# Staging of the last batch's h1 and h2 weights in two places by turns, in a two-layer transformer kernel

## The reference, cut to what matters

```python
def _L1_ffn_ref(x, w1_w, w1_s, w2_w, w2_s, h1_w, h1_s, h2_w, h2_s, w3_w, w3_s):
    h = silu(_tlin(x, w1_w, w1_s)) * _tlin(x, w2_w, w2_s)   # 256 -> 1024
    h = gelu(_tlin(h, h1_w, h1_s), approximate=False)       # 1024 -> 1024
    h = gelu(_tlin(h, h2_w, h2_s), approximate=False)       # 1024 -> 1024
    return _tlin(h, w3_w, w3_s)                             # 1024 -> 256
```

## Time and profile before

| What | Value |
|---|---|
| Median of 3 runs | 2720.88 us |
| The runs | 2719.23, 2720.88, 2723.3 us |
| The profiled execution's own time | 2726.29 us |
| Its span | 2724.6 us |
| Mean granted clock of TensorE in it | 0.927 |
| Busy, of the span | PE 86%, DVE 64%, ACT 55%, POOL 45% |
| Instructions | 27484 |
| Share of the DMA engines, queue q1 | 46.0%, 355.80 MB |

### The profile page before, as it was taken

The page is one execution under the profiler, slowest core; times in us unless marked ns, Lnnn a source line. Parts: engine busy times, 40 slices in busy tenths (PEclk is TensorE's granted clock), DMA queues, the critical chain, the costliest instruction groups (busy, mean ns, idle before and its releaser), DMA issues.

```text
span 2724.6 us, 27484 instructions
## 1 busy us (share of the span) xinstructions
PE 2330.2 (86%) x8452; PEld 1465.7 (54%) x8452; DVE 1748.2 (64%) x2782; ACT 1505.2 (55%) x1982; POOL 1226.2 (45%) x974
## 2 busy tenths in 40 slices
PE   2898989989989846778998998988988988998977
PEld 1456656567566622234554555555555555565666
DVE  3445464555454337899679679689689689687620
ACT  0232433425324225547877876876867866877733
POOL 1232251332422214556556556565556555556622
PEclk6899999999999867888999999998999999999988
DMA  7034534454445533444655645645645544647522
GB/s 227 0 119 137 166 124 133 150 162 132 136 137 155 174 110 108 119 117 131 171 133 131 170 133 134 171 132 129 175 129 134 171 128 138 160 133 176 151 83 78
DMA packets 381907, 374.34 MB, mean 137 GB/s; under 512 B 22369, under 2 KB 308593, under 8 KB 381761
## 3 DMA queue, kind: packets, MB, share of 16 engines
q1 hardware_dynamic: 375616, 355.80, 46.0%
q0 software_dynamic: 6144, 16.79, 2.0%
HBM read 335.45 MB, written 37.06 MB: 137 GB/s over the span
## 4 chain that ended last, share of the span: by engine, by line
PE 20%; DVE 13%; issue 11%; ACT 9%; DMA 6%; POOL 4%; SPq 1%; DVEq 0%; POOLq 0%; ACTq 0%
DMA w_stage<-h_T 5%; PE bank L1441 5%; PE bank L223 4%; DVE bank L1366 4%; PE bank L229 4%; PE bank L230 4%; DVE w_st L1374 4%; POOL d_in L1356 2%; ACT w_ring L1597 2%; ACT bank L1421 2%; DVE cv L1192 2%; ACT L1421 2%; PE bank L1674 1%; POOL f1L L1543 1%; PE bank L1675 1%
## 5 line engine op out<-in xcount | busy, mean ns | idle before, releaser
L1356 POOL TENSOR_TENSOR d_in<-u,bc 128x512 f32<-128x512 f32 x512 | 665.5, 1314 | 452.2 <-DMA bc<-bc_rows 327.7
L1366 DVE TENSOR_TENSOR_SCAN bank<-bank,d_in 128x512 f32<-128x512 f32 x512 | 624.7, 1221 | 185.7 <-ACT bank L1421 156.9
L1441 PE MATMUL bank<-w_st,ident 128*128 128x512 f32 x1024 | 544.8, 646 | 120.2 <-DVE w_st L1374 120.1
L1421 ACT ACTIVATE bank<-dt,a_neg 128x512 f32<-128x512 f32 x512 | 348.4, 687 | 292.9 <-DVE w_st L1374 291.0
L229 PE MATMUL bank<-f1H,w_ring 128*128 128x512 f32 x768 | 355.2, 462 | 34.8 <-POOL f1L L1543 23.8
L1441 PEld LDWEIGHTS bank<-w_st,ident 128*128 128x128 f32 x1024 | 194.2, 201 | 353.9 <-DVE w_st L1374 226.6
L1374 DVE TENSOR_TENSOR w_st<-bank,bc 128x512 f32<-128x512 f32 x512 | 343.9, 673 | 53.0 <-PE bank L1441 52.8
L230 PE MATMUL bank<-f1L,w_ring 128*128 128x512 f32 x768 | 311.3, 405 | 0.0
L229 PE MATMUL bank<-f0H,w_ring 128*128 128x512 f32 x512 | 230.2, 450 | 11.2 <-POOL f0L L1543 5.9
L1597 ACT ACTIVATE w_ring<-w_stage 128x1024 fp32r<-128x1024 f32 (+1 forms) x192 | 173.0, 905 | 112.6 <-DMA w_stage<-h_T 50.9
L1543 POOL TENSOR_TENSOR f0L<-mid,f0H 128x512 fp32r<-128x512 f32 x128 | 170.6, 1334 | 134.6 <-ACT f0H L1626 78.7
(11 more groups left out here) (202 smaller groups left out, 3898.5 us busy)
## 6 DMA issues: line engine op xcount, KB each, us to landing
bc<-bc_rows SPq DMA_DIRECT2D x256, 512.0 KB, 5.1
w_stage<-h_T SPq DMA_DIRECT2D x256, 256.0 KB, 3.4
w_exp<-L_ffn_ew SPq DMA_DIRECT2D x240, 256.0 KB, 4.6
w_stage<-w_T SPq DMA_DIRECT2D x128, 128.0 KB, 2.8
eo_rows<-eo SPq DMA_DIRECT2D x56, 256.0 KB, 4.3
xs<-xs_rows SPq DMA_DIRECT2D x24, 512.0 KB, 4.0
xA<-L_attn_x SPq DMA_DIRECT2D x8, 512.0 KB, 6.4
x_mid<-xA SPq DMA_DIRECT2D x8, 512.0 KB, 2.9
```

The costliest lines, as they stand in the source:

```text
L1356: pool.tensor_tensor(d_in[:, nth(b, s) % IN, :], u[:, c, :], rows_tile(b, use)[:, 0, :], ALU.mult).then_inc(in_made.sem, 1)
L1366: dve.tensor_tensor_scan(bank[:, :], bank[:, :], d_in[:, nth(b, s) % IN, :], 0.0, ALU.mult, ALU.add).then_inc(scanned.sem, 1)
L1421: act.activation(state_bank(b, s)[:, :], dt[:, c, :], ACT.Exp, scale=a_neg[:, c, n:n + 1]).then_inc(dA_made.sem, 1)
L1441: pe.matmul(y_bank(c)[:, :], ident[:, :], w_st[:, nth(b, s) % WG, :], start=False, stop=(n == NST - 1)).then_inc(summed.sem, 1)
```

## The change

For the last batch (`b == B - 1`) and the hidden steps (w >= 8), even steps are staged in `w_stage` as before and odd steps in `late_stage`, the first two thirds of `d_in`. The DMAs of step w then wait for the cast of w - 2 instead of w - 1 (step 8 still waits for all casts of the first eight, step 9 for the last scan of the batch), and their due time is that of the cast of w - 2. Both DMAs of a step count on the semaphore of its place. The other seven batches are issued as before.

```diff
@@ -1465,8 +1465,16 @@
 
 
 
-            def stage_part(w):
-                return w_stage[:, 4 * (w % 2):4 * (w % 2) + 4, :] if w < KF else w_stage[:, :, :]
+
+            late_stage = d_in[:, 0:2, :].rearrange("p a s -> p (a s)").rearrange("p (k n) -> p k n", n=P)
+
+            def by_turns(b, w):
+                return b == B - 1 and w >= KF
+
+            def stage_part(b, w):
+                if w < KF:
+                    return w_stage[:, 4 * (w % 2):4 * (w % 2) + 4, :]
+                return late_stage if by_turns(b, w) and w % 2 else w_stage[:, :, :]
 
             def ring_part(w):
                 if w < KF:
@@ -1477,6 +1485,8 @@
 
                 if w < KF:
                     return [stage_in[w % 2].at(b, 32 * (w // 2 + 1))]
+                if by_turns(b, w):
+                    return [stage_in[w % 2].at(b, 32 * KF // 2 + 32 * ((w - KF) // 2 + 1))]
                 return [stage_in[j].at(b, 32 * KF // 2 + 16 * (w - KF + 1)) for j in range(2)]
 
             def ring_freed(b, w):
@@ -1497,8 +1507,12 @@
                     yield 0
                     sp.dma_start(w3_stage, k_tiles(ins["w3_T"])).then_inc(w3_in.sem, 16)
                 for w in range(3 * KF):
-                    yield cast_at(b, w - (2 if w < KF else 1)) + PLAN["stage"]
-                    if w >= KF:
+                    yield cast_at(b, w - (2 if w < KF or by_turns(b, w) else 1)) + PLAN["stage"]
+                    if w == KF + 1 and by_turns(b, w):
+                        sp.wait_ge(*scanned.all(b))
+                    elif w > KF + 1 and by_turns(b, w):
+                        sp.wait_ge(*ring_made.at(b, w - 1))
+                    elif w >= KF:
                         sp.wait_ge(*ring_made.at(b, w))
                     elif w >= 2:
                         sp.wait_ge(*ring_made.at(b, w - 1))
@@ -1507,12 +1521,13 @@
                     m = slice(w % KF * P, (w % KF + 1) * P)
                     if w < KF:
                         for j, name in enumerate(("w1_T", "w2_T")):
-                            sp.dma_start(stage_part(w)[:, KD * j:KD * (j + 1), :], k_tiles(ins[name])[:, :, m]
+                            sp.dma_start(stage_part(b, w)[:, KD * j:KD * (j + 1), :], k_tiles(ins[name])[:, :, m]
                                          ).then_inc(stage_in[w % 2].sem, 16)
                     else:
                         for j in range(2):
                             k = slice(KF // 2 * j, KF // 2 * (j + 1))
-                            sp.dma_start(w_stage[:, k, :], k_tiles(ins[f"h{w // KF}_T"])[:, k, m]).then_inc(stage_in[j].sem, 16)
+                            there = stage_in[w % 2 if by_turns(b, w) else j]
+                            sp.dma_start(stage_part(b, w)[:, k, :], k_tiles(ins[f"h{w // KF}_T"])[:, k, m]).then_inc(there.sem, 16)
 
             def out_sync(b):
                 yield mlp_at(b) + 40
@@ -1594,7 +1609,7 @@
                         act.wait_ge(*there)
                     if b or w >= 4:
                         act.wait_ge(*ring_freed(b, w))
-                    act.activation(ring_part(w), stage_part(w), ACT.Copy).then_inc(ring_made.sem, 1)
+                    act.activation(ring_part(w), stage_part(b, w), ACT.Copy).then_inc(ring_made.sem, 1)
 
             def mlp_scalar(b):
                 M = mlp_at(b)
```

## The result

The changed kernel took 2702.9 us in the median of 4 runs (2698.73 to 2704.74), the kernel before 2720.12 in the median of 4 beside it; the ratio is 0.9932, with a 95% interval of 0.9915 to 0.995. The profiled execution took 2703.35 us with a span of 2701.6.

What follows compares the result with a forecast made beforehand. One staging place with a serial round was taken to bound the last batch's hidden steps: 25.4 + 2.9 + 5.4 + 25.4 + 2.9 = 62.0 us against 76.4. Gain 14.4, less 2.1 for luck, gave 2708.6 us, range 2703 to 2714.

Steps and rivals of the forecast that it cites:

- The mechanism: Last batch's hidden steps: the staging round of 4.82 us exceeds a 3.63 us tile; DMAs one cast earlier remove the landing.
- The queue of SP: Last batch: step 8's DMAs go ahead of the gbM load, moving it from 2618.0 to about 2621.7; cost nothing.
- The sum: First hidden tile after the opening one to last product: 62.0 us against 76.4, gain 14.4, with 5.4 for h2's first tile.
- Against the median: Whole kernel: half of 4.2 us taken off as the profiled execution's luck, so gain 12.3 and 2708.6 us.
- the late landing: Round before the cast for h1's last tile: 6.08 us instead of 4.82, counted as 1.26 us of luck.
- T7's clock: Last tile of h1, partly at 1.2 GHz: 5.36 us instead of 3.63, counted as 1.73 us of luck.
- T8's longer spell: First tile of h2, longer at 1.2 GHz: 6.62 us against 5.38, counted as 1.24 us of luck.
- Short pauses cost no clock: Rival: h2's first tile takes 3.63 us instead of 5.38 after its pause, time 2706.9; chance 0.12.
- Landings that share the engines: Rival: two steps in flight double each landing, 4.0 us a tile, 5 us given back, 2713.6; chance 0.07.
- ScalarE's order: Rival: odd casts behind two tiles' Gelus come late, PE waits at 7 odd tiles, 8.4 us back, 2717.0; chance 0.06.
- a clock that falls under steady load: Rival: hidden tiles without pauses run at 1.2 GHz, 3.0 us more each; with six, 2726.6; chance 0.03.
- no effect: Rival: last batch's DMAs still go out one at a time, held by SP's queue, 2720.9; chance 0.02.

Runs made afterwards that it cites:

- one_in_flight: Changed kernel, two staging places by turns, but each step's DMAs wait for the cast of w - 1 as before; 2723.01 us, ratio 1.0002 to the kernel before.
- h1_only: Changed kernel with staging by turns only for the eight steps of h1, h2 staged as before; 2716.92 us, ratio 0.9976 to the kernel before.
- no_landing: Changed kernel without the last batch's hidden-step DMAs from w = 10 on, casts using what lies in the two places; 2707.32 us in one run.
- before_again: The kernel before, unchanged, run again beside the unchanged changed kernel on one chip; 2720.7 us in the median of 12 runs.

## Why the prediction was right or wrong, point by point

**The mechanism was right.** The round of one step in flight set the hidden part; one_in_flight, h1_only and no_landing show it from three sides. From T1 to the last product 62.0 us were worked out, and 60.3, 61.9 and 60.3 measured. The waits of the earlier trace rows are gone, T1 to T7 and T9 to T14 take 3.63 us each, and the slack of ScalarE's odd cast is 1.2 us as worked out.

**One reading of the rows was wrong**, without a cost. The landing's 5% of the chain, 5.4% more exactly, is 147 us of 2724.6, and "nearly all of that" cannot lie in the last 90 us; 45 us of it lie behind the last scan, the rest in the batches before. The round itself was read rightly.

**The queue of SP** cost nothing, as said. `gbM` started at 2613.9 and its reader ran at 2619.0, before T0. Its landing took 4.6 us instead of 3.1 behind step 8. Step 8's cast came 5.1 us after its issue (2612.94 to 2618.01), behind which step 9 and `gbM` were in flight, against 3.8 before; T0 was waiting for a low part anyway.

**The sum against the profiled execution** was 14.4 us, and 14.0 of its difference lie after the last scan. That they are so near is luck. The stretch that the sum is about, T1 to the last product, gained 16.1 us: T8 ran at full clock (3.76) where 5.4 had been put. The slower up tiles and the slower T0 of that execution, in which TensorE does the same in both programs, took 2.1 us back.

**The step that failed is "Against the median"**, and beside it the 5.4 us for T8 in the sum. Half of 4.2 us was taken off the gain as luck of the profiled execution. Of the three terms only the late landing came and went: the round before T7's cast lasted 6.08 us, in one_in_flight 6.3, in before_again 5.0. T7's clock (1.73) was no term: with T7 at full clock the pause before T8 grew by as much, since the Gelus stood behind a cast in its round. T8's longer spell (1.24) was a term, but not luck: T8 took 6.62, 6.23 and 6.55 us in the three executions with the old round and order, and the cast for T10 waited for its end. So from T1 to the last product the kernel before took 76.4 and 73.8 us, 75.1 in the mean, where the halving makes it 74.3 (one_in_flight took 76.2). In the kernel after, T8 took 3.76, 5.35 and 3.76 us, and from T1 to the last product it is 60.8 in the mean instead of 62.0. The gain of this stretch is 14.3 us, not 12.3: 0.8 of the difference by the halving, 1.2 by the after side, nearly all of it T8. Slow spells in the up tiles, in T0 and in the last product, which differ from execution to execution, took 0.7 back, and 13.6 are left at the end of the span. That is 1.3 us of the 4.9 by which the gain was missed.

**The other 3.6 us, and the miss of the range, lie outside the stretch**, as far as the profiles show. The edges of the range were drawn with the distances of the lowest and the highest of three runs (1.7 and 2.4 us), while 29 runs of the same kernel, on one chip, lay between 2714.65 and 2733.67. With a spread of that size the lower edge would have stood several us lower. The later medians of the kernel after, 2709.19 and 2705.34, lie inside the range, and the later gains, 13.5 and 12.4, are near the forecast's 12.3. Which of the medians comes out is chance to that extent, for the forecast as well as against it.

**The rivals.** Short pauses cost no clock: half true. After the same pause of 2.70 us T8 ran at full clock in two executions and at 1.2 GHz for a part of it in one, while T0, after 3.48, had a slow spell in all three (6.3 us, 5.4 and 6.3). The last product, after 2.69 us, had one in two of the three (its 64 matmuls took 9.15, 7.64 and 9.16 us). The Trainium skill, "TensorE: Matmul & The Clock Gate", section "Why this matters for your kernels", warns of longer pauses only; the spells after 2.16 to 2.70 us differ from it, and the sum, which counted on a spell at T8 each time, was too firm the other way. The chance of 0.12 was too small. Landings that share the engines, ScalarE's order, a clock that falls under steady load, and no effect: each is refuted by the tiles of 3.63 at a clock of 1.00.

## What to carry to other kernels

Where a transfer waits for the buffer that its predecessor fills and the cast waits for the transfer, compare the round with what the consumer needs; if the round is longer, a second place is worth the difference for every item. A slow spell of the consumer is a term beside it only where the round in turn waits for the consumer, as the cast for T10 did for T8 and none did for T7. Before a term is called luck and halved, ask what it would turn into if it were gone (T7's slow clock would only have become a longer pause), and look for it in a second profile. And take the spread of a time from more than three runs, and the gain from the stretch that the change touches, which here repeated within 3.1 us while the whole repeated within 19.

## What the runs showed of the hardware that had not been expected

A pause of 2.70 us in the same place of the same program was followed by 2.4 GHz in two executions and by a spell at 1.2 GHz in one. Over the last batch of all 13 profiles, the 3 us behind a pause of TensorE had a granted clock of 0.50 to 0.73 after each pause of 3.0 us and more (35 of them), of 1.00 after each of 0.76 to 1.10 us, and the one or the other after those of 2.1 to 2.7 us (low in 11 of 18). Matmuls that nobody reads, put into the pauses, held 1.00 for 90 us and took 6.6 us off the end. A program of 2.7 ms with one core's work repeated its untouched first 2570 us only within 19 us over 13 executions, taken on at least three chips.
